# Order of TensorE's work in a selective-scan kernel: C spread first, convolution in three steps, sums of weights from ScalarE

## What is computed

```python
u = silu(conv(in_proj_w @ ctx) + conv_b)
delta = softplus(dt_proj_w @ dt_lo + dt_proj_b)        # dt_lo, B, C from x_proj_w @ u
state = state * exp(delta * A) + (delta * u) * B[n]    # for 16 states n, along 256 steps of time
y = sum_n(state[n] * C[n]) + D * u
x1 = x + y * silu(layernorm(x))
p = softmax(layernorm(x1) @ Wg);  gates, experts = top_k(p, 2)
out = x1 + sum_k(gates[k] * (relu(rows @ w1[e]) @ w2[e]))   # each expert takes its first 320 rows
```

## Time and profile before

| | |
|---|---|
| time of three runs | 288.33, 289.02, 290.1 us; median 289.02 |
| the profiled execution | 288.53 us, span 286.7 us |
| busy share | TensorE 84%, weight loads 76%, VectorE 75%, ScalarE 61%, GpSimd 74% |
| mean granted TensorE clock | 0.93 |
| chain that ended last | TensorE 39%, issue 4%, VectorE 4%, DMA 2%, GpSimd 2%, ScalarE 1% |

### The profile page before, as it was taken

The page is one execution under the profiler, slowest core; times in us unless marked ns, Lnnn a source line. Parts: engine busy times, 40 slices in busy tenths (PEclk is TensorE's granted clock), DMA queues, the critical chain, the costliest instruction groups (busy, mean ns, idle before and its releaser), DMA issues.

```text
span 286.7 us, 5022 instructions
## 1 busy us (share of the span) xinstructions
PE 239.6 (84%) x1564; PEld 218.4 (76%) x1564; DVE 216.1 (75%) x372; ACT 174.1 (61%) x379; POOL 213.5 (74%) x174
## 2 busy tenths in 40 slices
PE   8967597867957396678699999999999999999970
PEld 7745476545845285557589999999999999999960
DVE  3799999999799999999978757566675738383620
ACT  2899759777886776669326357463747465564400
POOL 1689899669976999998744668687777777777561
PEclk9999959995999957589999999999999999999995
DMA  6679520080002805043032675745544454544110
GB/s 158 236 224 330 215 120 0 5 305 25 0 1 67 303 0 187 0 145 112 21 129 74 205 235 186 231 169 205 174 178 169 178 173 179 213 181 182 38 59 24
DMA packets 15073, 40.38 MB, mean 141 GB/s; under 512 B 2922, under 2 KB 9900, under 8 KB 12112
## 3 DMA queue, kind: packets, MB, share of 16 engines
q1 hardware_dynamic: 11792, 33.15, 33.9%
q0 software_dynamic: 2816, 6.32, 6.6%
q10 hardware_dynamic: 448, 0.70, 0.9%
HBM read 32.72 MB, written 8.49 MB: 144 GB/s over the span
## 4 chain that ended last, share of the span: by engine, by line
PE 39%; issue 4%; DVE 4%; DMA 2%; POOL 2%; ACT 1%; POOLq 1%; SPq 0%; ACTq 0%
PE ps L1064 12%; PE ps L1065 11%; PE ps L1066 11%; DVE h L1291 2%; PE ps L1073 2%; PE ps L1080 2%; DVE hc L1303 1%; DMA xe<-expert_rows 1%; DMA expert_rows<-xrow,sloti 1%; POOL expert_rows L403 1%; POOL so_far L482 1%; POOL out L491 1%; DMA out<-eo,dst 1%; POOLq L108 1%; DVE eo L1497 0%
## 5 line engine op out<-in xcount | busy, mean ns | idle before, releaser
L358 POOL TENSOR_TENSOR dbu<-du,bsb 128x1024 f32<-128x1024 f32 x31 | 72.7, 2366 | 1.2 <-DMA bsb<-b_rows 1.0
L582 ACT ACTIVATE ps<-delta,anegs 128x255 f32<-128x255 f32 x128 | 53.0, 461 | 14.4 <-DVE h L1284 10.7
L1486 DVE SCALAR_TENSOR_TENSOR htlo<-ps,hthi 128x320 fp32r<-128x320 f32 x64 | 30.4, 487 | 37.8 <-ACT hthi L748 37.8
L847 PE MATMUL ps<-stack,sels 64*128 64x256 f32 x64 | 17.2, 355 | 34.9 <-DVE hc L1303 32.1
L847 PEld LDWEIGHTS ps<-stack,sels 64*128 64x128 f32 x64 | 11.0, 215 | 42.7 <-issue 42.3
L472 POOL TENSOR_TENSOR w2lo<-w2raw,w2hi 128x512 fp32r<-128x512 f32 x28 | 35.9, 1302 | 9.0 <-ACT w2hi L643 8.8
L869 PE MATMUL ps<-cst,hc 128*128 128x128 f32 x256 | 40.7, 310 | 1.4 <-DVE hc L1303 1.4
L1284 DVE TENSOR_TENSOR_SCAN h<-ps,dbu 128x1024 f32<-128x1024 f32 x18 | 41.1, 2283 | 0.4 <-POOL dbu L358 0.3
L1064 PE MATMUL ps<-xthi,w1hi 128*128 (+1 forms) x124 | 39.3, 317 | 0.3 <-ACT w1hi L636 0.3
L748 ACT ACTIVATE hthi<-ps 128x320 fp32r<-128x320 f32 x64 | 28.0, 437 | 18.6 <-PE ps L1066 18.6
L1303 DVE TENSOR_TENSOR hc<-h,ps 128x1024 f32<-128x1024 f32 x31 | 37.1, 1197 | 2.6 <-issue 2.0
(11 more groups left out here) (185 smaller groups left out, 510.4 us busy)
## 6 DMA issues: line engine op xcount, KB each, us to landing
w1raw<-in_w SPq DMA_DIRECT2D x8, 1024.0 KB
w2raw<-in_w SPq DMA_DIRECT2D x8, 1024.0 KB, 4.9
bsb<-b_rows SPq DMA_DIRECT2D x7, 1024.0 KB, 6.6
expert_rows<-fill SPq DMA_DIRECT2D x1, 2580.0 KB, 15.8
xe<-expert_rows SPq DMA_DIRECT2D x8, 258.0 KB, 5.1
out<-x SPq DMA_DIRECT2D x4, 256.0 KB, 5.1
xnat<-in_x SPq DMA_DIRECT2D x1, 768.0 KB, 7.3
xe<-expert_rows SPq DMA_DIRECT2D x8, 64.5 KB, 5.2
```

Of the source, the lines that this page charges most:

```text
L358: nc.gpsimd.tensor_tensor(dbu[j % DRING][:], du[:, :, None, cols(b)].to_broadcast([P, EC, 2, L]), bsb[b % 2][:, None, 2 * p:2 * p + 2, :]. ...
L582: ins = nc.scalar.activation(decays(g % SLOTS_DA)[:, c, i * L + 1:(i + 1) * L], delta[:, c, b * L + 1:(b + 1) * L], ACT.Exp, scale=anegs[: ...
L1486: nc.vector.scalar_tensor_tensor(out=htlo[:, f, :], in0=ps[:, f % 4, 0:CAP], scalar=0.0, in1=hthi[:, f, :].bitcast(F32), op0=ALU.max, op1= ...
```

## The change

1. TensorE issues `c_cast(g + 1)` at the head of a step, ahead of `logits` and `counts`.
2. The convolution goes out in steps p = 3, 4 and 5: three taps of the first half; the fourth tap and two of the second half; the last two taps.
3. The second bank of C holds step 30 and no longer step 31. VectorE does product 30 ahead of scan 31. Six added zeros (`add_zeros`, L878, two records each) follow the sums of step 30.
4. ScalarE's exponential of the top logits also gives their sum (`accum_out`). VectorE's `sum_weights` and ScalarE's `weigh` are gone. GpSimd takes the reciprocal as a power of -1 and multiplies the gates, for batch 0 ahead of the drive of step 21, for batch 1 ahead of that of step 30, for batch 2 behind W1's low pieces, for batch 3 where it made the gates before.

```diff
 def c_bank(g):
-    return WBANK if g == STEPS - 1 else CBANK
+    return WBANK if g == STEPS - 2 else CBANK
...
+            def weigh(b):
+                pool.wait_ge(s["top_exp"], b + 1)
+                pool.wait_ge(s["const_done"], 1)
+                tiles = tiles_of(b)
+                nc.gpsimd.tensor_tensor(rsum[:, tiles], rsum[:, tiles], none1[:, tiles], ALU.pow
+                                        ).then_inc(s["sum_inverse"], 1)
+                pool.wait_ge(s["sum_inverse"], b + 1)
+                nc.gpsimd.tensor_tensor(xrow[:, tiles, :, DM], etop[:, tiles, 0:TOPK],
+                                        rsum[:, tiles, None].to_broadcast([P, BT, TOPK]), ALU.mult
+                                        ).then_inc(s["gates_done"], 1)
...
                 if b == 2 and p in (1, 5):
                     if p == 1:
                         pool.wait_ge(s["xe_filled"], 16)
+                        weigh(0)
                     send(0 if p == 1 else 1)
+                if b == 3 and p == 2:
+                    weigh(1)
                 if b == 3 and p in (2, 3):
                     send(p)
                 drive(j)
...
+            weigh(B - 2)
             for j in tiles_range(B - 2):
                 send(j)
...
             pool.wait_ge(s["xe_in"], 32)
-            pool.wait_ge(s["weights_sum"], B)
-            for j in tiles_range(B - 1):
-                ins = nc.gpsimd.tensor_scalar(xrow[:, j, :, DM], etop[:, j, 0:TOPK], rsum[:, j:j + 1], None, ALU.mult)
-            ins.then_inc(s["gates_done"], 1)
+            weigh(B - 1)
...
                     ins = nc.scalar.activation(etop[:, j, :], top[:, j, :], ACT.Exp, bias=ntop[:, j:j + 1],
-                                               scale=rx[:, j:j + 1])
+                                               scale=rx[:, j:j + 1], accum_out=rsum[:, j:j + 1])
...
-                    if p == (5 if b == B - 1 else 7):
-                        weigh(b - 1)
...
-            def conv(b, c, bank):
+            def conv(b, c, bank, taps=range(TAPS)):
...
-                if g == STEPS - 1:
+                if g == STEPS - 2:
                     pe.wait_ge(s["zt_done"], B)
+                elif g == STEPS - 1:
+                    pe.wait_ge(s["mult_done"], g - 1)
                 elif g:
                     pe.wait_ge(s["mult_done"], g)
...
+                if g + 1 < STEPS - 1:
+                    c_cast(g + 1)
+                if g == STEPS - 3:
+                    c_cast(STEPS - 1)
                 if b >= 1:
                     if p == (3 if b == B - 1 else 4):
                         logits(b - 1)
                     if p == (4 if b == B - 1 else 6):
                         counts(b - 1)
-                if g + 1 < STEPS - 1:
-                    c_cast(g + 1)
-                if g == STEPS - 3:
-                    c_cast(STEPS - 1)
...
-                if b == B - 1 and p in (2, 3, 4, 5):
+                if b == B - 1 and p in (2, 3, 4, 5, 6):
...
-                    add_zeros((4, 4, 6, 2)[p - 2])
+                    add_zeros((4, 4, 6, 2, 6)[p - 2])
...
-                if b + 2 < B and p in (3, 4):
+                if b + 2 < B and p == 3:
                     pe.wait_ge(s["sp_t"], nb + 1)
-                    conv(b + 2, p - 3, WBANK)
+                    conv(b + 2, 0, WBANK, range(0, 3))
+                if b + 2 < B and p == 4:
+                    conv(b + 2, 0, WBANK, range(3, TAPS))
+                    conv(b + 2, 1, WBANK, range(0, 2))
+                if b + 2 < B and p == 5:
+                    conv(b + 2, 1, WBANK, range(2, TAPS))
...
-                if g + 1 < STEPS:
+                if g < STEPS - 2:
                     scan(g + 1)
-                mult(g)
+                    mult(g)
+                else:
+                    mult(g)
+                    if g + 1 < STEPS:
+                        scan(g + 1)
...
-                    if p == (5 if b == B - 1 else 7):
-                        sum_weights(b - 1)
```

More of the change, by code:

```diff
@@ L129, in build @@
         nhalf = sb("nhalf", [P, TILES])
+        none1 = sb("none1", [P, TILES])
         stats = sb("stats", [P, TILES, 6])
@@ L218, in build @@
             "ones_made ctx_in0 ctx_in inp_in dts_in xps_in x_in0 x_in small_in sel_in sel_done w1_in w2_in xe_in fill_made mean_neg xe_zeroed xe_filled "
-            "cw_in ch_in cw_done const_done dtb_in skip_done opened weights_sum xe0_psum wdt_psum wdt_done cv_step cv_done conv_psum u_done "
+            "cw_in ch_in cw_done const_done dtb_in skip_done opened sum_inverse xe0_psum wdt_psum wdt_done cv_step cv_done conv_psum u_done "
             "xp_psum hi_done brow_done brow_out b_lo_in b_hi_in stack_done v_psum "
@@ L319, in _ @@
             nc.gpsimd.memset(nhalf[:], -0.5)
+            nc.gpsimd.memset(none1[:], -1.0)
             nc.gpsimd.memset(fill[:, 0:DM + 1], 0.0)
@@ L808, in first_dt @@
                 return ins
-            def conv(b, c, bank):
+            def conv(b, c, bank, taps=range(TAPS)):
                 acc = by_chunk(bank)[:, c, :]
-                for k in range(TAPS):
+                for k in taps:
                     ins = nc.tensor.matmul(acc[:, k:L], cwb[:, TAPS - 1 - k, c * P:(c + 1) * P],
@@ L815, in conv @@
                                            stop=(k == TAPS - 1), skip_group_check=True)
-                if c == EC - 1:
+                if c == EC - 1 and taps[-1] == TAPS - 1:
                     ins.then_inc(s["conv_psum"], 1)
@@ L1388, in place @@
                 nc.vector.tensor_copy(sloti[:, tiles, :], slot).then_inc(s["slots_done"], 1)
-            def sum_weights(b):
-                tiles = tiles_of(b)
-                dve.wait_ge(s["top_exp"], b + 1)
-                link(nc.vector.tensor_reduce(rsum[:, tiles], etop[:, tiles, :], AX.X, ALU.add))
-                nc.vector.reciprocal(rsum[:, tiles], rsum[:, tiles]).then_inc(s["weights_sum"], 1)
             def low_w1(e, m):
@@ L1453, in _ @@
             place(last)
-            sum_weights(last)
             def low_w2(e, m):
```

## The result

The changed kernel takes 293.49 us (median of four runs, 293.12 to 296.77), the kernel before 288.97 us beside it (288.33 to 290.1): a ratio of 1.0177, 95% interval 1.0098 to 1.0257. A second series, of six runs, gave 1.0181 (1.0133 to 1.0229). Ratios are taken over executions run side by side, without those in the chip's slower state, so they can differ from the quotient of the medians. The profiled execution took 293.12 us, 4.6 us above the profiled execution of before; its span is 291.1 us, 4.4 us above 286.7. The forecast was 4.0. A lower granted clock doesn't account for this: in the second series, executions with a mean granted clock of 0.916 to 0.92 took 292.96 and 293.52 us with the changed kernel, 288.75 and 290.23 us with the kernel before.

The account below looks back on a forecast made before the run. VectorE was taken to set the pace up to about 145 us, TensorE from about 153 us. Terms +0.7 - 0.1 + 1.05 + 2.35 = +4.0 us gave 293.0 us against the median of 289.02; range 290.0 to 295.6.

Parts of the forecast that it names:

- C spread first: TensorE in the scan stage: logits and counts behind C make VectorE wait at place and choose, 5.3 us in all.
- Batch 0: Scan 9: late convolution end delays ScalarE's silu and decay; +0.7 us and not -0.6.
- Batch 1: Product 13 to scan 17: 1.55 us less waiting, nearly all taken back by place; -0.1 us.
- Sums of weights, batch 2: Scan 25: GpSimd's added power and gate product, 1.05 us a batch, are not hidden; +1.05 us.
- GpSimd's path to scan 25 is 1.05 longer: Batch 2: GpSimd ends last, since VectorE's own path grows by only 0.45 us; the batch gives +1.05.
- Batch 3 and tail: VectorE from the last batch to expert 0: +2.75 us, less 0.4 as the placing is done beforehand; +2.35.
- rival 2: Clock falls in batch 3, where TensorE waits longer; choose and place cost some 2.5 us more: 295.5 us, chance 0.12.
- the zeros that fill its waits stay: Batch 3, TensorE: given, with a granted clock of 0.90 from 120 to 140 us, as evidence against a clock fall.
- Product 30 ahead of scan 31: End of the scan stage: the last gate's 0.9 us wait stays, product 31 about 0.1 dearer; +0.1 us.
- 1 (the side engines hide their part): Scan stage: ScalarE's decays are in time and GpSimd's pair is cheap; +1.7 us, 290.7 us, chance 0.2.
- 3 (the expert stage absorbs it): Expert stage: experts 0 and 1 wait for weights anyway, so all 4.0 us go: 289.0 us, chance 0.05.
- 4: Batch 1: product 13 waits as before, so the batch gives +1.1 and not -0.1: 294.2 us, chance 0.05.

Follow-up runs that it names:

- weights of batch 0 earlier: The changed kernel with GpSimd's weights of batch 0 moved ahead of its add of x of batch 1: 294.73 us, ratio 1.0163.

## Why the prediction was right

The time came out as forecast (293.49 against 293.0), the sum as well (+4.56 against +4.0 us), and the mechanism that carried most of it is the one named. Its terms stand closer in sum than one by one: batch 0 was off by 0.07 us, batch 1 by -0.83, batch 2 by +0.66, batch 3 with the tail by +0.66. That the sum is off by only 0.56 is in part luck, and so is which execution was profiled: the second profile of the changed kernel has +5.84.

- **C spread first.** Right. Three waits of place and one of choose, each the price of C and of the counts or logits in one piece. From the product's end I had 1.27 for place of batches 0 and 1, 1.55 for choose of batch 2 and 1.4 for its place; they were 1.16 and 1.26, 1.64 and 1.37. By itself the part brings 6.02 us of such waits, 3.69 of them net in the profiled execution.
- **Batch 0** (+0.7, measured +0.77). Right, with its chain: the silus start late behind the third piece (1.55 us of waiting), the decays behind them, and scan 9 waits 1.29, for which I had 1.2. That silus of z put first take the wait away shows that the chain is this one. Its size hangs on the half clock, which I had taken over from the kernel before: where the first piece of the convolution took 2.07 us and not 2.76 (weights of batch 0 earlier, the same program up to there), scan 9 waits 0.48 and batch 0 is 21.14 us long, no longer than before.
- **Batch 1** (-0.1, measured -0.93). The term that was mis-sized is the waiting that I left: 0.45 us at product 13 and 0.4 at scan 17 for ScalarE's decay; neither is there. I had half clock from the spread and the sums ahead of the taps on, as before, and C out at 72.4 us, 18.6 behind gate 0. In the changed kernel the clock fell later. The sums ahead of the taps took 1.09 us (1.97 at 67.35 before). The taps themselves took 2.67 us, as forecast (three quarters of 3.60), but they started earlier, and C is out at 72.16, 17.75 behind gate 0:

```profile
67.40:68.70 1.30, 1.26 (x10) 1.16 (x11) 1.30 (x2) 0.72 (x3) 1.30 (x1) 1.00 0.00 0
...
69.50:71.30 1.80, 1.80 (x5) 1.01 (x3) 1.80 (x3) 1.72 (x5) 1.80 (x2) 0.50 0.00 0
```

```profile
67.84 1.09 PE L875 MATMUL ps<-cst,hc 128*128 128x128 f32 x8
...
68.77 2.67 PE L817 MATMUL ps<-ctxs,cwb 128*128 128x256 f32 x6
...
71.37 0.79 PE L853 MATMUL ps<-stack,sels 64*128 64x256 f32 x2
72.10 1.12 PE L907 MATMUL ps<-wgs,xnt 128*128 128x8 f32 x8
...
72.77 1.20 DVE L1314 TENSOR_TENSOR hc<-h,ps 128x1024 f32<-128x1024 f32 x1
```

  The other half of the term held: place took back 1.16 us of the 2.00 that product 13 no longer waits. C's order has its share in it: with three pieces but the logits still ahead of C, product 13 waited 0.85.
- **Sums of weights, batch 2** (+1.05, measured +1.71). The pair was put at 1.05 us for GpSimd, a power of 0.73 and a product of 0.29 with 0.03 between. It takes 0.72, 0.08 of gap, 0.21; that is right. What failed is the step "GpSimd's path to scan 25 is 1.05 longer": the indirect DMA behind the pair waits for the product:

```profile
91.35 0.72 POOL L403 TENSOR_TENSOR rsum<-rsum,none 128x2 f32<-128x2 f32 x1
92.15 0.21 POOL L406 TENSOR_TENSOR xrow<-etop,rsum 128x4 f32<-128x4 f32 x1
93.28 1.25 POOL L417 DMA_INDIRECT expert_rows<-xrow,sloti  x1 [0.92 <-POOL xrow L406]
```

  0.92 us, where the same DMA had 0.19 before, and I priced none. It starts 6.25 us behind gate 1, before 4.54: that is the batch's +1.71. The trace of before held the same wait, 0.8 us, in the last batch, where GpSimd made the gates; I had not read it there. So scan 25, which waited 0.29, waits 0.87:

```profile
117.45 2.29 DVE L1295 TENSOR_TENSOR_SCAN h<-ps,dbu 128x1024 f32<-128x1024 f32 x1 [0.87 <-POOL dbu L360]
```

  The Trainium skill's "GPSIMD Engine Reference", section 4.1 Engine selection, puts GpSimd at about twice VectorE's time for elementwise work on two inputs. Here the power took 0.72 us where VectorE's reciprocal, another operation, takes 0.166; of products and the like with two inputs of 128x2, one took 0.20 us on GpSimd (L460) and 0.16 on VectorE (L1374). The page's direction holds, its factor for neither pair of these small tiles. ScalarE's accumulated sum is an instruction of its own, 186 ns a tile, inside the bounds that I gave:

```profile
L633 ACT ACTIVATION_READ_ACCUMULATOR etop<-top,ntop,rx 128x1 f32 x8 | 1.5, 186 | 0.0
```

- **Batch 3 and tail** (+2.35, measured +3.26 - 0.25 = +3.01). The two waits were right (1.64 and 1.37). Not foreseen was a wait of product 30 for C, which TensorE could not spread in time, since zeros and turns at half clock stand ahead of it (the bracket names no releaser; the zeros took 1.50 us at full clock before):

```profile
140.37 2.62 PE L884 MATMUL ps<-onesf,fill 128*128 128x128 f32 x12
...
144.43 1.22 DVE L1314 TENSOR_TENSOR hc<-h,ps 128x1024 f32<-128x1024 f32 x1 [0.35 <-issue]
```

  From 140 to 144 us the granted clock was 0.57. So the clock did fall in batch 3, as rival 2 has it, but behind choose and place, whose price stayed that of full clock; it was dearer at the zeros that I had taken for cover ("the zeros that fill its waits stay"). The tail gave 0.25 back, not 0.4: the placed rows now start at 154.88 with no wait for their DMA, as said.
- **Product 30 ahead of scan 31** (+0.1). Right: the part alone gives +0.08 to expert 0, and the last gate still waits 0.82 us.
- **Rivals.** 1 (the side engines hide their part) is out: scans 9 and 25 both wait. 3 (the expert stage absorbs it) is out: 133.65 against 133.64 us. 4 is out: product 13 has no wait. 2 shows in part, as told.

What stays open: the worth of part 4 and of earlier weights in the whole time, and that of the convolution in three steps once C stands first, since the clock fell in other places in each execution that was to tell it.

## What to carry to other kernels

Where an in-order engine waits for another, the work ahead of the waiting instruction is free and that behind it is not. So before moving an instruction that waits to the front, list what was hidden in its wait, and who needs that next: four results that were needed directly behind the same event cost 1.2 to 1.6 us each here. When a wait comes from work at half clock, look first at the clock: with filler in TensorE's idle time ahead of that work, and the order of the work as it was, the kernel before became faster (ratio 0.9955), which no reordering here did.

## What the runs showed that I had not expected

- The stretch in which TensorE's granted clock falls to 0.5 (the lower of its two levels) differs between executions of one kernel. In the changed kernel the first taps of batch 1 took 2.67 us in one profile and 1.46 in the other, the zeros of step 28 2.62 and 1.50. That moves single waits by 0.3 to 1.4 us.
- The profiles fall into two kinds. In five (before, changed, and three variants) the granted clock was 1.00 from 20 to 24 us, scan 4 starts at 32.2 to 32.5 us, and from 36 to 42 us, at the first convolution, the clock was 0.50 to 0.55. In the other eight, the changed kernel's second among them, it was 0.50 to 0.59 from 20 to 24 us, scan 4 starts at 33.7 to 34.6, and from 36 to 42 us it was 0.59 to 1.00. A variant in one kind against a kernel in the other shows the clock's waits as if they were the variant's. So a part worth under about 1 us is read from its waits and the length of its stretch, in profiles where the clock fell alike.
- An indirect DMA on GpSimd that depends on GpSimd's own product waits 0.79 to 0.92 us for it, in every profile here; where it waits for nothing else its gap is 0.16 to 0.31 us.
